# Context of batches 1 to 7 loaded in 32-by-32 blocks and turned on VectorE

## The chip, the core and the metric

The kernel runs on one core of a Trainium2 chip. Its engines are TensorE (PE in the profile, with PEld for its weight loads), VectorE (DVE), ScalarE (ACT), GpSimd (POOL) and SyncE (SP), which here issues every DMA. The metric is the device time of one launch in microseconds, lower is better. Each engine runs its own instructions in order, and they wait for each other by semaphores.

## What is computed

One layer of cross-attention with a residual, then a gated sign-weight feed-forward with a residual. The stage that this change touches is the projection of the keys and values, whose input is the context and the normalised latents:

```python
hidden_states = jnp.concatenate([context, latents], axis=1)      # (8, 256, 512)
q = (latents @ Wq).reshape(b, q_len, N_KV_HEADS, N_GROUPS, HEAD_DIM)
k = (hidden_states @ Wk).reshape(b, kv_len, N_KV_HEADS, HEAD_DIM)
v = (hidden_states @ Wv).reshape(b, kv_len, N_KV_HEADS, HEAD_DIM)
scores = jnp.einsum('bqhgd,bkhd->bhgqk', q, k) * scale
attn = jax.nn.softmax(scores.astype(jnp.float32), axis=-1).astype(q.dtype)
out = jnp.einsum('bhgqk,bkhd->bqhgd', attn, v)
...
x = x + _L0_xattn_ref(_layernorm(x, axis=-1), ctx_4096, Wq, Wk, Wv, Wo)
x = x + _L0_ffn_ref(_layernorm(x, axis=-1), weight, bias, gate_w, in_scale, out_scale)
```

There are 8 batches of 128 context rows and 128 latent rows, 512 wide; 32 query heads and 4 key heads of 128.

## The kernel before

Everything is in fp32. A product is made from a high part (rounded to fp32r) and a low part (the rest) of both operands, with three of the four partial products: 12 matmuls of 128x512 for one product of the value projection.

The program has stages: the value projection ("V stage", up to about 61 us), the key projection ("K stage", to about 106 us), and then, for each key head and each half of its query heads, attention and output projection, with the feed-forward woven into the last round. The order of each engine is written out by hand; nothing is scheduled by a program.

In the V stage a batch `b` has two products, number `n = 2b` for the context (`cT`) and `n = 2b + 1` for the latents (`xT`). Both need their input with the features on the partitions, while memory has the rows there, so each is turned first:

- SP loads the raw context `craw[:, b]` (`load_c`, L244) and the raw latents `acc[:, b]` (`load_x`, L241), 256 KB each in 128 runs of 2 KB. The order on SP's queue is: `craw` 0, the first two quarters of Wv, `acc` 0, the other two quarters, then `craw` and `acc` of batches 1 to 7 in turn, with Wk (1 MB) after batch 4, then the gate weights and the bias, and only then the stores of V.
- PE turns the context with four transpositions against the identity into `t_bank[1]` (`ct_transpose`, L1105), and the normalised latents `y` into `t_bank[0]` (`xt_transpose`, L1097). Behind the context's product of batch `b` stands the context's transposition of `b + 1`, behind the latents' product the latents' transposition of `b + 1`.
- ACT copies the turned tile to the high part (`ct_half`, `xt_half`), DVE writes the rest (`ct_rest`, `xt_rest`). All such copies and subtractions go through two helpers and have the lines L563 (ACT) and L821 (DVE).
- PE makes the product (`product`, L1088) in one of two banks. ACT copies its high part into `v_stage`, DVE the rest, which raises `proj_lo`. Product `n` waits until the bank is free: `proj_lo` of product `n - 2`.
- After both products of a batch SP stores `v_stage[:, b % 2]` to `v_park` (L277). ACT may write a batch into `v_stage` only when the store of batch `b - 2` has landed: it waits for `v_parked` ahead of its first instruction of batch `b`, which is `ct_half(b + 1)`.
- DVE's order in batch `b` is: `ct_rest(b+1)`, layer statistics of `b + 2`, the rest of product `2b`; `xt_rest(b+1)`, layer norm of `b + 2`, the rest of product `2b + 1`. POOL makes 1/sqrt from the variance in six small instructions.

Of the kernel before, what the change touches and what calls it, by code (L numbers as in the profile page):

```python
# [22 lines left out]
HI, LO = 0, 1  # L23
# [4 lines left out]
def xattn_ffn(nc, x, ctx, wq, wk, wv, wo, ffn_w, ffn_b, gate_w, in_cs, out_cs, out):  # L28
# [6 lines left out]
    P = 128  # L35
    B, T, D = x.shape
    HC = D // P
# [16 lines left out]
    QB = P // 32  # L54

    es = ExitStack()
    with es:
        def sb(stack, name, shape, dt=fp32):
            return stack.enter_context(nc.sbuf_tensor(name, shape, dt))

        def sem(name):
            return es.enter_context(nc.semaphore(name))
# [39 lines left out]
        with ExitStack() as pre:  # L102
            cT = sb(pre, "cT", [P, 2, HC, B * T], f32r)
            wv_pair = sb(pre, "wv_pair", [P, 2, HC, D], f32r)
            craw = sb(pre, "craw", [P, B, D])
            wk_pair = sb(pre, "wk_pair", [P, 2, HC, D], f32r)
            v_stage = sb(pre, "v_stage", [P, 2, G, 2, KC, P], f32r)
            k_stage = sb(pre, "k_stage", [P, 2, HALF, 2, QB, KC, 32], f32r)

        with ExitStack() as att:  # L110
# [17 lines left out]
        with ExitStack() as fin:  # L128
# [9 lines left out]
        s_bank, t_bank, proj_bank = bank[0:2], bank[2:4], bank[6:8]  # L138
# [9 lines left out]
        c_in = [sem(f"c_in{b}") for b in range(B)]  # L148
# [17 lines left out]
            sem(n) for n in ("stats_ready", "mv_ready", "rstd_ready", "rstd_step", "shift_ready",  # L166
                             "y_ready"))

        xt_ready, xt_hi, xt_lo, ct_ready, ct_hi, ct_lo = (
            sem(n) for n in ("xt_ready", "xt_hi", "xt_lo", "ct_ready", "ct_hi", "ct_lo"))  # L170

        proj_ready, proj_hi, proj_lo = sem("proj_ready"), sem("proj_hi"), sem("proj_lo")

# [58 lines left out]
        def _(sp):  # L232
# [8 lines left out]
                sp.dma_start(acc[:, b, :], x[b]).then_inc(x_in[b], 16)  # L241

            def load_c(b):
                sp.dma_start(craw[:, b, :], ctx[b]).then_inc(c_in[b], 16)  # L244

            def load_wq(g, quad, c):
                cols = bass.ds(g * (QUADS * QH * P) + quad * QH * P, QH * P)
# [10 lines left out]
            def load_v(g, b):  # L258
                sp.dma_start(words(vg[:, b, :, :, :]), v_park[g, :, b, :, :, :]).then_inc(v_in[b], 16)

            load_c(0)
            for c in range(HC):
                if c == 2:
                    load_x(0)
                sp.dma_start(raw_a[:, c, :], wv[c * P:(c + 1) * P, :]).then_inc(wv_in[c], 16)
            for b in range(1, B):
                load_c(b)
                load_x(b)
                if b == 4:
                    sp.dma_start(raw_b[:, :, :], wk.rearrange("(c p) n -> p c n", p=P)  # L270
                                 ).then_inc(wk_in, 16)
# [287 lines left out]
        def _(act):  # L559
            open_loop(act, *exp_ready, p_hi, o_hi)  # L560

            def copy(dst, src):
                return nc.scalar.activation(dst, src, ACT.Copy)  # L563
# [9 lines left out]

            def ct_half(b):

                act.wait_ge(ct_ready, b + 1)
                copy(cT[:, HI, :, b * T:(b + 1) * T],
                     t_bank[1][:, :].rearrange("p (c t) -> p c t", c=HC)).then_inc(ct_hi, 1)

            for c in range(HC):  # L580
                act.wait_ge(wv_in[c], 16)
# [4 lines left out]
            for b in range(B):  # L586
                if b >= 2:
                    act.wait_ge(v_parked[b % 2], 16 * (b // 2))
                for kc in range(KC):
                    n = 2 * b + kc  # L590
# [17 lines left out]
            for u in range(G * NHALF):  # L608
                if 3 <= u < 6:
# [4 lines left out]
                    rows = slice(32 * (u - 3), 32 * (u - 3) + E)  # L614
# [3 lines left out]
                for kc in range(KC):  # L618
                    n = 2 * B + 2 * u + kc
# [197 lines left out]
        def _(dve):  # L817
            open_loop(dve, *max_ready, rsum_ready, *turned, o_lo, acc_ready)

            def subtract(dst, a, b):  # L820
                return nc.vector.tensor_tensor(dst, a, b, ALU.subtract)  # L821

            def layer_stats(i, b):
                nc.vector.bn_stats(stats[:, i % 2], acc[:, b, :]).then_inc(stats_ready, 1)  # L824
                dve.wait_ge(stats_ready, i + 1)
                nc.vector.bn_aggr(mv[:, i], stats[:, i % 2]).then_inc(mv_ready, 1)

            def layer_norm(i, b):

                dve.wait_ge(rstd_ready, 2 * i + 2)  # L830
                nc.vector.tensor_scalar(y[:, i % 2], acc[:, b, :], mv[:, i, 0:1], rstd[:, i:i + 1],
                                        ALU.subtract, ALU.mult).then_inc(y_ready, 1)

            def xt_rest(b):
                dve.wait_ge(xt_hi, b + 1)
                part = xT[:, :, :, b * T:(b + 1) * T]
                subtract(part[:, LO], t_bank[0][:, :].rearrange("p (c t) -> p c t", c=HC),
                         part[:, HI]).then_inc(xt_lo, 1)

            def ct_rest(b):  # L840
                dve.wait_ge(ct_hi, b + 1)
                part = cT[:, :, :, b * T:(b + 1) * T]
                subtract(part[:, LO], t_bank[1][:, :].rearrange("p (c t) -> p c t", c=HC),
                         part[:, HI]).then_inc(ct_lo, 1)

            ct_rest(0)
            dve.wait_ge(x_in[0], 16)
            layer_stats(0, 0)
            for c in range(HC):
                if c == 2:  # L850
# [4 lines left out]
                subtract(wv_pair[:, LO, c, :], raw_a[:, c, :], wv_pair[:, HI, c, :]  # L855
                         ).then_inc(wv_lo, 1)
            xt_rest(0)
            layer_norm(1, 1)
            for b in range(B):
                for kc in range(KC):  # L860
                    n = 2 * b + kc
                    if b + 1 < B:
                        (ct_rest, xt_rest)[kc](b + 1)
                    if b + 2 < B:
                        if kc == 0:
                            dve.wait_ge(x_in[b + 2], 16)
                            layer_stats(b + 2, b + 2)
                        else:
                            dve.wait_ge(xt_ready, b + 1)
                            layer_norm(b + 2, b + 2)  # L870
                    dve.wait_ge(proj_hi, n + 1)
                    subtract(v_stage[:, b % 2, :, LO, kc, :],
                             proj_bank[n % 2][:, :].rearrange("p (g d) -> p g d", g=G),
                             v_stage[:, b % 2, :, HI, kc, :]).then_inc(proj_lo, 1)
            for u in range(G * NHALF):
# [4 lines left out]
                for kc in range(KC):  # L880
                    n = 2 * B + 2 * u + kc
# [191 lines left out]
        def _(pe):  # L1073
# [19 lines left out]
            def xt_transpose(b):  # L1093
                pe.wait_ge(y_ready, b + 1)
                pe.wait_ge(xt_lo, b)
                for c in range(HC):
                    last = nc.tensor.transpose(t_bank[0][:, c * T:(c + 1) * T],  # L1097
                                               y[:, b % 2, c * P:(c + 1) * P], ident[:, :])
                last.then_inc(xt_ready, 1)
# [11 lines left out]
            for b in range(B):  # L1111

                for kc, (src, lo_sem) in enumerate(((cT, ct_lo), (xT, xt_lo))):
                    n = 2 * b + kc
                    if n == 0:
                        pe.wait_ge(ct_hi, 1)
                    else:
                        pe.wait_ge(lo_sem, b + 1)
                    if n >= 2:
                        pe.wait_ge(proj_lo, n - 1)  # L1120
                    product(proj_bank[n % 2][:, :],
                            lambda s, c: src[:, s, c, b * T:(b + 1) * T],
                            lambda s, c: wv_pair[:, s, c, :], HC,
                            (wv_hi, wv_lo) if n == 0 else None,
                            {1: lambda: pe.wait_ge(ct_lo, 1), 2: lambda: xt_transpose(0)}
                            if n == 0 else {}
                            ).then_inc(proj_ready, 1)
                    if b + 1 < B:
                        (ct_transpose, xt_transpose)[kc](b + 1)

            pe.wait_ge(gate_in, 16)
            pe.wait_ge(xt_lo, B)
# [6 lines left out]
            for u in range(G * NHALF):  # L1139

                g, half = divmod(u, NHALF)
                for kc, src in enumerate((cT, xT)):
                    n = 2 * B + 2 * u + kc
# [227 lines left out]
```

## Time and profile before

| | us |
|---|---|
| median of 3 runs | 694.87 (694.29 to 695.62) |
| the profiled execution, its own time | 695.12 |
| its span, first to last instruction | 693.3 |
| PE busy in the span | 672.2 (97%) |
| DVE / ACT / POOL busy | 444.4 / 354.7 / 304.5 |

The times below are counted from the span's start. In the rows, a line of the timeline is start, duration, engine, line, operation, what is written from what; in brackets the idle time before it and what ended it. SPq is the queue of SP: the duration there is that of the issue, not of the transfer.

### The profile page before, as it was taken

The page shows a single profiled execution, that of the slowest core. Times are in us where ns is not written, and L with a number is a line of the kernel's source. Part 1 is how long each engine was busy: PE and PEld are TensorE (multiplying, and loading weights), DVE is VectorE, ACT ScalarE, POOL GpSimd, SP SyncE. Part 2 cuts the span into 40 slices and gives each one's busy share as a digit, 9 for nine tenths or more (in the row PEclk, how much of TensorE's full clock was granted, in tenths as well). Part 3 has the DMA queues.
Part 4 walks back from the last instruction along what each step waited for, and adds up shares of the span by engine and source line. Part 5 has one row for each costly group of instructions (what it writes and reads, how often), then busy time and mean ns, then how long its engine had stood idle before and what let it go on. Part 6 is the DMA issues. An engine that isn't in the chain of part 4 may idle for free.

```text
span 693.3 us, 10261 instructions
## 1 busy us (share of the span) xinstructions
PE 672.2 (97%) x3368; PEld 563.6 (81%) x3368; DVE 444.4 (64%) x726; ACT 354.7 (51%) x889; POOL 304.5 (44%) x272
## 2 busy tenths in 40 slices
PE   6999999999999999999999999999999999989995
PEld 4888887878888888888888888888888888768774
DVE  4553233666776766777767777667766676667763
ACT  3344322755565456555655564465556545646542
POOL 4135000542374246324633463345236438854773
PEclk9999999999999999999999999999999999999998
DMA  9556447689668876656698866667877665454411
GB/s 322 216 206 242 197 197 251 200 259 265 202 183 269 264 252 202 222 187 182 198 289 256 243 207 198 194 185 249 260 253 238 190 191 206 166 141 139 146 46 45
DMA packets 90692, 144.84 MB, mean 209 GB/s; under 512 B 15192, under 2 KB 47960, under 8 KB 89616
## 3 DMA queue, kind: packets, MB, share of 16 engines
q1 hardware_dynamic: 90640, 144.19, 64.9%
q8 instruction: 27, 0.44, 0.3%
q14 instruction: 25, 0.20, 0.1%
HBM read 91.60 MB, written 52.56 MB: 208 GB/s over the span
## 4 chain that ended last, share of the span: by engine, by line
PE 86%; DMA 4%; DVE 3%; POOL 2%; ACT 2%; issue 1%; SPq 1%; ACTq 0%; DVEq 0%
PE bank L1088 47%; PE bank L1202 23%; PE bank L1187 11%; DMA p_park<-p_turned 2%; PE bank L1278 2%; POOL p_low L459 1%; DMA kg<-k_park 1%; DVE bank L929 1%; DMA acc<-in_x 1%; POOL wo_pair L473 1%; ACT prob L646 1%; PE bank L1097 1%; DVE stats L824 1%; PE bank L1252 1%; PE bank L1237 1%
## 5 line engine op out<-in xcount | busy, mean ns | idle before, releaser
L459 POOL TENSOR_TENSOR p_low<-p_low,p_high 128x1024 fp32r<-128x1024 f32 x64 | 153.8, 2403 | 252.3 <-ACT p_high L563 252.2
L1202 PE MATMUL bank<-wo_pair,oT 128*128 128x512 f32 x768 | 188.5, 393 | 4.3 <-DVE oT L821 3.3
L1088 PE MATMUL bank<-xT,wq_pair 128*128 128x512 f32 x768 | 185.7, 391 | 0.0
L1202 PEld LDWEIGHTS bank<-wo_pair,oT 128*128 128x128 f32 x768 | 139.3, 188 | 34.2 <-issue 5.7
L1088 PEld LDWEIGHTS bank<-xT,wq_pair 128*128 128x128 f32 x768 | 140.2, 188 | 26.8
L563 ACT ACTIVATE oT<-bank 128x512 fp32r<-128x512 f32 x64 | 38.3, 598 | 197.4 <-DVE bank L929 197.4
L646 ACT ACTIVATE prob<-bank,nmax 128x256 f32<-128x256 f32 x256 | 119.1, 471 | 32.7 <-DVE nmax L899 32.5
L914 DVE STREAM_TRANSPOSE p_turned<-prob 128x512 f32<-128x512 f32 x128 | 91.0, 711 | 61.1 <-ACT prob L646 61.1
L1088 PEld LDWEIGHTS bank<-kg,qT 128*128 128x128 f32 x768 | 108.0, 190 | 11.5 <-DMA kg<-k_park 1.2
L1088 PE MATMUL bank<-kg,qT 128*128 128x256 f32 x768 | 111.6, 283 | 1.5 <-DMA kg<-k_park 0.8
L899 DVE TENSOR_REDUCE nmax<-bank 128x2 f32<-128x512 f32 x128 | 87.6, 686 | 38.3 <-PE bank L1088 38.3
L929 DVE TENSOR_TENSOR bank<-bank,r_all 128x512 f32<-128x512 f32 x64 | 69.0, 1078 | 39.2 <-PE bank L1187 39.2
L1187 PE MATMUL bank<-p_high,vg 128*128 128x512 f32 x256 | 69.0, 391 | 0.0
L563 ACT ACTIVATE p_high<-p_low 128x1024 fp32r<-128x1024 f32 x64 | 67.7, 1057 | 0.2
L467 POOL TENSOR_TENSOR wq_pair<-raw_a,wq_pair 128x512 fp32r<-128x512 f32 x28 | 36.4, 1300 | 58.7 <-ACT wq_pair L563 58.7
L1187 PEld LDWEIGHTS bank<-p_high,vg 128*128 128x128 f32 x256 | 47.6, 188 | 9.6
L921 DVE TENSOR_TENSOR acc<-bank,acc 128x512 f32<-128x512 f32 x64 | 44.2, 690 | 12.8 <-PE bank L1202 12.8
L646 ACT ACTIVATION_READ_ACCUMULATOR prob<-bank,nmax 128x1 f32 x256 | 50.4, 197 | 0.0
L892 DVE SCALAR_TENSOR_TENSOR qT<-bank,qT 128x512 fp32r<-128x512 f32 x64 | 43.6, 682 | 10.3 <-ACT qT L634 10.1
L821 DVE TENSOR_TENSOR oT<-bank,oT 128x512 fp32r<-128x512 f32 x64 | 44.1, 689 | 4.1
L634 ACT ACTIVATE qT<-bank 128x512 fp32r<-128x512 f32 x64 | 37.9, 593 | 10.7 <-PE bank L1088 10.7
L473 POOL TENSOR_TENSOR wo_pair<-raw_b,wo_pair 128x512 fp32r<-128x512 f32 x32 | 40.5, 1302 | 0.2 <-ACT wo_pair L563 0.2
(89 smaller groups left out, 601.0 us busy)
## 6 DMA issues: line engine op xcount, KB each, us to landing
p_park<-p_turned SPq DMA_DIRECT2D x64, 512.0 KB, 3.7
p_low<-p_park SPq DMA_DIRECT2D x64, 512.0 KB, 4.9
r_all<-r_park SPq DMA_DIRECT2D x64, 256.0 KB, 4.5
v_park<-v_stage SPq DMA_DIRECT2D x8, 1024.0 KB, 4.1
raw_a<-in_L_xattn_Wq SPq DMA_DIRECT2D x32, 256.0 KB, 5.2
raw_b<-in_L_xattn_Wo SPq DMA_DIRECT2D x32, 256.0 KB, 4.9
k_park<-k_stage SPq DMA_DIRECT2D x8, 1024.0 KB, 3.8
kg<-k_park SPq DMA_DIRECT2D x32, 256.0 KB, 5.4
```

Of the source, the lines that this page charges most:

```text
L459: nc.gpsimd.tensor_tensor(part, part.bitcast(fp32), p_high[:, :].rearrange("p i c q -> p (i c q)"), ALU.subtract).then_inc(p_lo, 1)
L473: nc.gpsimd.tensor_tensor(wo_pair[:, LO, h, :], raw_b[:, h, :], wo_pair[:, HI, h, :], ALU.subtract).then_inc(wo_lo, 1)
L563: return nc.scalar.activation(dst, src, ACT.Copy)
L646: ins = nc.scalar.activation(prob[:, p, j], s_bank[p][:, j * KEYS:(j + 1) * KEYS], ACT.Exp, bias=nmax[:, p, j:j + 1], accum_out=esum[:, t ...
L821: return nc.vector.tensor_tensor(dst, a, b, ALU.subtract)
L899: nc.vector.tensor_reduce(nmax[:, p], s_bank[p][:, :].rearrange("p (h k) -> p h k", h=2), AX.X, ALU.max, negate=True).then_inc(max_ready[p ...
L914: nc.vector.transpose(p_turned[:, t % 2, :, 2 * p:2 * p + 2, :].rearrange("p k h q -> p h k q"), prob[:, p].rearrange("p h (k e) -> p h k ...
L921: nc.vector.tensor_tensor(acc[:, t], wo_bank[:, :], acc[:, t], ALU.add).then_inc(acc_ready, 1)
L929: nc.vector.tensor_tensor(o, o, r_all[:, t % 2].rearrange("p (i q) h -> p i h q", i=QB), ALU.mult).then_inc(o_scaled, 1)
L1088: last = nc.tensor.matmul(dst, left(a, c), right(b, c), start=(n == 0), stop=(n == 3 * chunks - 1))
L1187: last = nc.tensor.matmul(av_bank[:, :], vg[:, t, vs, kc, :], ps[:, :, kc, :], start=(n == 0), stop=(n == 3 * KC - 1))
L1202: last = nc.tensor.matmul(wo_bank[:, :], oT[:, s, h, :], wo_pair[:, w, h, :], start=((s, w) == TERMS[0] and h == 0), stop=((s, w) == TERMS ...
```

## The change

The context of batch 0 is loaded and turned as before. For batches 1 to 7:

- the load takes 32-by-32 blocks to where a turn inside each block completes the whole transposition. It is four DMAs per batch, one for each group of 32 partitions, each of 32 x 16 runs of 32 floats (128 bytes). The bytes are the same.
- PE's `ct_transpose(b)` is gone; DVE has a new instruction `ct_turn(b)`, one transposition of 128x512 in 32x32 blocks from `craw` to a new tile `cturn` (two batches deep, 2 KB a partition each).
- ACT's `ct_half` and DVE's `ct_rest` read `cturn` in place of the PSUM bank. `ct_turn(1)` stands ahead of the second layer norm, `ct_turn(b + 2)` right behind `ct_rest(b + 1)`.

`cturn` shares its memory with `k_stage`, which is first written in the K stage.

```diff
             def load_c(b):
-                sp.dma_start(craw[:, b, :], ctx[b]).then_inc(c_in[b], 16)
+                if b == 0:
+                    sp.dma_start(craw[:, b, :], ctx[b]).then_inc(c_in[b], 16)
+                    return
+
+
+                blocks = ctx[b].rearrange("(k s) (c i r) -> i s c k r", s=32, i=QB, r=32)
+                for i in range(QB):
+                    rows = craw[32 * i:32 * (i + 1), b, :].rearrange("s (c k r) -> s c k r", c=HC, k=QB)
+                    sp.dma_start(rows, blocks[i]).then_inc(c_in[b], 16)
...
             def ct_half(b):
 
-                act.wait_ge(ct_ready, b + 1)
-                copy(cT[:, HI, :, b * T:(b + 1) * T],
-                     t_bank[1][:, :].rearrange("p (c t) -> p c t", c=HC)).then_inc(ct_hi, 1)
+                if b == 0:
+                    act.wait_ge(ct_ready, 1)
+                    src = t_bank[1][:, :]
+                else:
+                    act.wait_ge(ct_turned, b)
+                    src = cturn[:, b % 2]
+                copy(cT[:, HI, :, b * T:(b + 1) * T], src.rearrange("p (c t) -> p c t", c=HC)
+                     ).then_inc(ct_hi, 1)
...
+            def ct_turn(b):
+                dve.wait_ge(c_in[b], 16 * QB)
+                nc.vector.transpose(cturn[:, b % 2].rearrange("p (m s) -> p m s", s=32),
+                                    craw[:, b].rearrange("p (m r) -> p m r", r=32)
+                                    ).then_inc(ct_turned, 1)
+
...
             xt_rest(0)
+            ct_turn(1)
             layer_norm(1, 1)
             for b in range(B):
                 for kc in range(KC):
                     n = 2 * b + kc
                     if b + 1 < B:
                         (ct_rest, xt_rest)[kc](b + 1)
+                        if kc == 0 and b + 2 < B:
+                            ct_turn(b + 2)
...
-                    if b + 1 < B:
-                        (ct_transpose, xt_transpose)[kc](b + 1)
+                    if kc == 1 and b + 1 < B:
+                        xt_transpose(b + 1)
```

On SP's queue, at the start of the program, before (`craw` is the raw context, `acc` the raw latents):

```order
L244 DMA craw<-in_ctx 128x512
L265 DMA raw_a<-in_L_xattn_Wv 128x512 x2
L241 DMA acc<-in_x 128x512
L265 DMA raw_a<-in_L_xattn_Wv 128x512 x2
L244 DMA craw<-in_ctx 128x512
L241 DMA acc<-in_x 128x512
```

and now:

```order
L248 DMA craw<-in_ctx 128x512
L276 DMA raw_a<-in_L_xattn_Wv 128x512 x2
L244 DMA acc<-in_x 128x512
L276 DMA raw_a<-in_L_xattn_Wv 128x512 x2
L255 DMA craw<-in_ctx 32x16x32 x4
L244 DMA acc<-in_x 128x512
```

Each context load from batch 1 on is four issues in place of one, and everything on the queue behind it stands 3 issues further back for each batch.

On PE, around the first context product of a batch (rows with `y` are the latents' transposition), before:

```order
L1088 MATMUL bank<-wv_pair,xT 128x512 x11
L1097 MATMUL bank<-ident,y 128x128 [waits xt_lo,y_ready]
L1097 MATMUL bank<-ident,y 128x128 x3
L1088 MATMUL bank<-wv_pair,cT 128x512 [waits proj_lo,ct_lo]
L1088 MATMUL bank<-wv_pair,cT 128x512 x11
L1105 MATMUL bank<-ident,craw 128x128 [waits ct_lo,c_in2]
L1105 MATMUL bank<-ident,craw 128x128 x3
```

and now:

```order
L1114 MATMUL bank<-wv_pair,xT 128x512 x11
L1123 MATMUL bank<-ident,y 128x128 [waits xt_lo,y_ready]
L1123 MATMUL bank<-ident,y 128x128 x3
L1114 MATMUL bank<-wv_pair,cT 128x512 [waits proj_lo,ct_lo]
L1114 MATMUL bank<-wv_pair,cT 128x512 x11
L1114 MATMUL bank<-wv_pair,xT 128x512 [waits proj_lo,xt_lo]
```

The two rows of L1105 are gone, and the latents' product follows the context's product directly.

On DVE, from the end of the first batch's preparation (`xT` of batch 0) to the rest of the first product (`v_stage`), before:

```order
L821 TENSOR_TENSOR xT<-bank,xT 128x4x128 [waits xt_hi]
L831 TENSOR_SCALAR y<-acc,mv,rstd 128x512 [waits rstd_ready]
L821 TENSOR_TENSOR cT<-bank,cT 128x4x128 [waits ct_hi]
L824 BN_STATS stats<-acc 128x6 [waits x_in2]
L826 BN_AGGR mv<-stats 128x2 [waits stats_ready]
L821 TENSOR_TENSOR v_stage<-bank,v_stage 128x4x128 [waits proj_hi]
```

and now:

```order
L837 TENSOR_TENSOR xT<-bank,xT 128x4x128 [waits xt_hi]
L858 STREAM_TRANSPOSE cturn<-craw 128x512 [waits c_in1]
L847 TENSOR_SCALAR y<-acc,mv,rstd 128x512 [waits rstd_ready]
L837 TENSOR_TENSOR cT<-cturn,cT 128x4x128 [waits ct_hi]
L858 STREAM_TRANSPOSE cturn<-craw 128x512 [waits c_in2]
L840 BN_STATS stats<-acc 128x6 [waits x_in2]
L842 BN_AGGR mv<-stats 128x2 [waits stats_ready]
L837 TENSOR_TENSOR v_stage<-bank,v_stage 128x4x128 [waits proj_hi]
```

Two turns stand ahead of the first `v_stage` row, and one more ahead of each later one of a context product.

## Rows read from the trace of the kernel before

**Rows 1.** The page, part 4: the chain that ended last, share by engine.
```profile
PE 86%; DMA 4%; DVE 3%; POOL 2%; ACT 2%; issue 1%; SPq 1%; ACTq 0%; DVEq 0%
```

**Rows 2.** The chain in order of time, start of program: start, duration, what.
```profile
4.00 5.72 DMA acc<-in_x
...
9.75 0.70 DVE stats L824
...
11.15 0.78 PE bank L1097 x4
...
13.34 3.05 PE bank L1088 x12
16.40 0.44 PE bank L1097 x4
16.83 2.78 PE bank L1088 x12
19.61 0.44 PE bank L1105 x4
```

**Rows 3.** The timeline of 12 to 16 us, DVE and ACT.
```profile
12.60 0.69 DVE L821 TENSOR_TENSOR xT<-bank,xT 128x512 fp32r<-128x512 f32 x1 [0.30 <-ACT xT L563]
...
13.24 0.55 DVE L831 TENSOR_SCALAR y<-acc,mv,rstd 128x512 f32<-128x512 f32 x1
...
13.84 0.59 ACT L563 ACTIVATE v_stage<-bank 128x512 fp32r<-128x512 f32 x1
13.98 0.69 DVE L821 TENSOR_TENSOR cT<-bank,cT 128x512 fp32r<-128x512 f32 x1 [0.19 <-ACT cT L563]
14.58 0.69 DVE L824 BATCH_NORM_STATS2 stats<-acc 128x6 f32<-128x512 f32 x1
...
15.40 0.66 DVE L821 TENSOR_TENSOR v_stage<-bank,v_stage 128x512 fp32r<-128x512 f32 x1
```

**Rows 4.** The page, part 5: DVE's block transposition of the attention stage.
```profile
L914 DVE STREAM_TRANSPOSE p_turned<-prob 128x512 f32<-128x512 f32 x128 | 91.0, 711 | 61.1 <-ACT prob L646 61.1
```

**Rows 5.** The timeline, SP's queue: issues of one context load, bias, V stores.
```profile
3.53 0.43 SPq L244 DMA_DIRECT2D craw<-in_ctx  x1
...
12.22 0.35 SPq L273 DMA_DIRECT2D bias_b<-in_L_ffn_bias  x1
...
19.27 19.70 SPq L277 DMA_DIRECT2D v_park<-v_stage  x4
```

**Rows 6.** DMA issues of 3.5:3.9, 12.2:12.6, 19.1:20 us; last number: us to landing.
```profile
craw<-in_ctx SPq DMA_DIRECT2D x1, 256.0 KB, 5.5
...
bias_b<-in_L_ffn_bias SPq DMA_DIRECT2D x1, 256.0 KB, 8.6
...
v_park<-v_stage SPq DMA_DIRECT2D x1, 1024.0 KB, 4.1
```

**Rows 7.** DMA queue of 124.5:124.9, 127.0:127.6, 14:19 us: packets, MB, share of 16 engines.
```profile
DMA packets 86, 0.00 MB, mean 3 GB/s; under 512 B 86, under 2 KB 86, under 8 KB 86
...
q1 hardware_dynamic: 86, 0.00, 12.1%
...
DMA packets 199, 0.20 MB, mean 340 GB/s; under 512 B 0, under 2 KB 199, under 8 KB 199
...
q1 hardware_dynamic: 199, 0.20, 98.4%
...
q1 hardware_dynamic: 1092, 2.03, 105.0%
```

**Rows 8.** Stretches at the end: PE, PEld, DVE, ACT, POOL busy, PEclk, DMA share, GB/s.
```profile
680.00:682.00 2.00, 0.21 (x1) 0.18 (x1) 1.57 (x4) 0.82 (x3) 1.44 (x2) 0.61 0.29 109
682.00:684.00 2.00, 1.63 (x6) 1.35 (x6) 0.55 (x2) 0.28 (x1) 0.00 (x0) 0.50 0.00 0
684.00:686.00 2.00, 2.00 (x6) 1.53 (x5) 1.05 (x2) 1.09 (x2) 0.00 (x0) 0.50 0.00 0
686.00:688.00 2.00, 2.00 (x7) 1.59 (x7) 0.53 (x2) 0.00 (x0) 0.00 (x0) 0.68 0.00 0
```

More of the change, by code:

```diff
@@ L107, in xattn_ffn @@
             v_stage = sb(pre, "v_stage", [P, 2, G, 2, KC, P], f32r)
+            with ExitStack() as turned_ctx:
+                cturn = sb(turned_ctx, "cturn", [P, 2, D])
             k_stage = sb(pre, "k_stage", [P, 2, HALF, 2, QB, KC, 32], f32r)
@@ L167, in xattn_ffn @@
                              "y_ready"))
-        xt_ready, xt_hi, xt_lo, ct_ready, ct_hi, ct_lo = (
-            sem(n) for n in ("xt_ready", "xt_hi", "xt_lo", "ct_ready", "ct_hi", "ct_lo"))
+        xt_ready, xt_hi, xt_lo, ct_ready, ct_turned, ct_hi, ct_lo = (
+            sem(n) for n in ("xt_ready", "xt_hi", "xt_lo", "ct_ready", "ct_turned", "ct_hi", "ct_lo"))
         proj_ready, proj_hi, proj_lo = sem("proj_ready"), sem("proj_hi"), sem("proj_lo")
@@ L842, in ct_rest @@
                 part = cT[:, :, :, b * T:(b + 1) * T]
-                subtract(part[:, LO], t_bank[1][:, :].rearrange("p (c t) -> p c t", c=HC),
-                         part[:, HI]).then_inc(ct_lo, 1)
+                src = t_bank[1][:, :] if b == 0 else cturn[:, b % 2]
+                subtract(part[:, LO], src.rearrange("p (c t) -> p c t", c=HC), part[:, HI]
+                         ).then_inc(ct_lo, 1)
             ct_rest(0)
```

## The prediction

> **What bounds the kernel now.** I read the chain that ended last first: 86% of the span is PE's [rows 1], and in order of time the V stage is one line of PE pieces without a gap from 13.34 us on: product, four transpositions, product, four transpositions [rows 2]. A removed piece of that line is time won, if nothing else comes late. A transposition of four costs the line 0.44 us, a product 2.78 us; a product that starts after a wait costs 3.05 us, 0.27 more, since the array fills again (I use 0.25). Before 13.34 us the chain is not PE's: it runs through the landing of the latents of batch 1 at 9.72 us (4.00 + 5.72), DVE's statistics behind it, the first layer norm, the transposition of `xT` at 11.15. So the start is bound by the DMA queue.
>
> **What a load costs on the queue.** The context of batch 1 lands at 3.53 + 5.5 = 9.03 us and the bias at 12.22 + 8.6 = 20.82 [rows 5, 6]. Between them lie 13 loads of 256 KB, Wk (four times as much) and the bias: 18 units in 11.79 us, 0.655 us each, and the engines are never free in between (105.0% for 14 to 19 us) [rows 7]. The change leaves the bytes and makes 2048 packets of 128 bytes, 128 for each of 16 DMA engines, out of 128 packets of 2 KB, 8 for each. The trace of before has no packet of that size. Its neighbours: 86 packets of at most 16 bytes took 12.1% of 0.4 us x 16 = 0.77 us, 9.0 ns each; 199 packets of 1 KB took 98.4% of 0.6 x 16 = 9.45 us, 47.5 ns each [rows 7]. An eighth of a 1 KB packet shouldn't take longer than the whole, so 9.0 and 47.5 ns are the bounds. The straight line between them gives 9.0 + 112 x 38.5 / 1008 = 13.3 ns. I take that, as 128 bytes are much nearer to the 16-byte row. A context load then costs 128 x 13.3 ns, plus four times 9 ns for the semaphore packets of its four DMAs, 1.74 us: 1.09 us more than now, seven times.
>
> The trace's own rows thus make the small runs about 2.7 times as slow as the long ones. The Trainium skill says in "DMA: Bandwidth & Descriptors", section "Specifications", that a transfer reaches line rate from 512 bytes on, and that below this the engine does a read-modify-write. No row shows or denies that. It speaks against this change, and what it would do here is the second rival below.
>
> **The change part by part.**
>
> 1. *Transpositions gone from PE.* Seven times four. The first (batch 1) gives nothing: after it PE waited for `xT` of batch 0, which DVE had at 13.29 (12.60 + 0.69), and started at 13.34 [rows 2, 3]. It turns into waiting. The other six stand between products without a gap: 6 x 0.44 = 2.64 us won.
>
> 2. *First latents later.* The load of batch 1's context stands ahead of the latents of batch 1, on which the chain waits at 9.72. They land 1.09 us later, and the whole of PE's line with them: 1.09 us lost. Issue isn't the limit there: three more issues of 0.43 us plus 0.04 end at 4.9 us, while their data starts to move at about 8.4.
>
> 3. *DVE's turns.* Seven at 0.71 us, the price of the same operation on the same size in attention [rows 4]. In a batch of 6.0 us DVE has some 4 us of work, so the sum fits; what matters is the order. In batch 0 two of them stand ahead of the rest of product 0. Walk through it, 1.09 later than now: `xT` rest done 14.38, turn 1 to 15.1, ACT's `ct_half(1)` from 15.1 instead of ahead of 13.84, so its copy of product 0 ends at 16.2. DVE: `ct_rest(1)` 15.7, turn 2 16.3, statistics 16.95, rest of product 0 from 17.8 to 18.5 (now 15.40 to 16.06 [rows 3]). Product 2 waits for it: PE is ready at 14.43 + 3.05 + 0.44 = 17.92 and starts at 18.51. Lost: 0.59 + 0.25 to fill again = 0.84 us. From batch 1 on the turn is one batch ahead of its use, and the same walk leaves 0.4 us or more of slack.
>
> 4. *The V stores behind the loads.* This is the largest term. The store of batch 0 now is issued at 19.27 and lands 4.1 us later at 23.37, right behind the bias (20.82 plus 1 MB) [rows 5, 6]. The queue is first in, first out, so with seven loads of 1.09 more it lands at 23.37 + 7.63 = 31.0. ACT may not begin batch 2 before it: behind that wait stand `ct_half(3)` and the copy of product 4; on DVE behind those `ct_rest(3)`, turn 4, statistics 4, rest of product 4. Now that store lands before ACT gets there and the wait costs nothing. After: ACT's two copies 31.0 to 32.0, with DVE's `ct_rest(3)` from 31.65, turn 4 32.25, statistics 32.9 and 33.6, rest of product 4 from 33.75 to 34.43: 3.45 us after the landing. Product 6 needs that bank. PE is ready at 18.51 + 3.05 + 2.79 + 0.44 + 2 x 2.79 + 0.44 = 30.81 and starts at 34.47. Lost: 3.66 + 0.25 = 3.91 us. Later stores land in time: the next one is right behind (33.6, used by ACT about then), the queue is empty after that. SP's 21 more issues at 0.47 end at 12.6 + 9.9 = 22.5, past the 19.27 at which V's store is ready, but the data ahead of it moves until 28.4, which hides that.
>
> 5. *The clock.* It is granted in full through the V stage. At the end it fell, in a stretch with PE busy for 0.21 us of 2, and stood at half (1.2 in place of 2.4 GHz) for 2 x (0.78 + 1 + 1 + 0.64) = 6.8 us of four stretches [rows 8]. A wait of 3.7 us is as empty. There PE kept waiting after the fall; here it goes on at once, so I take half of that, 3.4 us at half clock, in which products that take 1.6 to 2 times as long lose about 1.5 us.
>
> ACT's and DVE's reads from `cturn` instead of PSUM are of equal size and hidden. After the V stage nothing changes, and PE's line carries the difference to the end (the K stage has no DMA or DVE wait).
>
> Sum: -2.64 + 1.09 + 0.84 + 3.91 + 1.5 = +4.7 us. On the profiled execution's own 695.12 us this gives 699.8; that execution is 0.25 us above the median of the runs, less than the doubt in any term.
>
> **Rivals.**
>
> *Cheap packets: the change doesn't lose, and ends below the time before.* If a 128-byte packet costs the lower bound of 9.0 ns, a load costs 1.19 us, 0.53 more. The latents come 0.53 late, term 3 stays 0.84, the store lands at 27.1, and product 6 could start at 30.6 where PE is ready at 30.25: 0.35 + 0.25. No clock loss. -2.64 + 0.53 + 0.84 + 0.60 = -0.7, 694.4 us. It decides at about 9.6 ns a packet, where the sum is zero; each nanosecond on top costs 0.128 x 8 = 1.0 us. For it: small packets in the trace do go at 9.0 ns; against: those carry 16 bytes, and the size has a price in every other row.
>
> *Dear packets.* If small reads cost double (26.6 ns), a load costs 3.44 us, 2.8 more; the store lands at 42.9, product 6 starts at 46.4 where PE is ready at 32.5. -2.64 + 2.8 + 0.84 + 14.1 + 1.5 = +16.6, 711.7 us. At the upper bound of 47.5 ns it is +36, 731 us. For it: the 16-byte packets are writes, and reads from memory may not overlap as well in small pieces. Against: the 2 KB reads lie on the line of the other two rows to within 3 ns (1092 packets of 14 to 19 us took 84 us; of them 991 of 2 KB, 83.9 ns each, where the line gives 86.6) [rows 7]. The Trainium skill's read-modify-write below 512 bytes ("DMA: Bandwidth & Descriptors", "Specifications"), taken as twice the price, would end here too.
>
> *No clock loss.* All as forecast, but the wait leaves the clock alone: +3.2, 698.3 us.
>
> **How the numbers follow.** Forecast with or without the clock loss, 11 to 17 ns a packet: 0.55 (+1.5 to +8.5 us). Cheap packets, below 11 ns: 0.17, of which most within 0.2% (1.4 us, about what a measurement of this kernel can tell from no change) and hardly any below, since even the cheapest case wins only 0.7: 0.14 same, 0.03 faster. Dear packets, above 17 ns: 0.28, half of it below 26. Slower 0.83. The range takes in the lower bound's 694.4 and reaches into the dear case to 712.
>
> **What would show it.** Context loads landing 1.1 us further apart from each other; the first `xT` transposition on PE at 12.2 instead of 11.15; a wait of PE of 0.6 us ahead of product 2 (about 18 us) and one of 3 to 4 us at about 31 us, with ACT waiting for the V store just before and PEclk below 1 behind it; batches of 6.0 us after that. Wrong would be the forecast if the wait at 31 us is missing (packets under 10 ns) or over 8 us long (twice the price), or if waits stand in every batch, which would be DVE or the context loads and not the store.

## The result: 707.62 us, 1.8% slower, and the profile after

| | before | changed |
|---|---|---|
| median of 4 runs, us | 694.58 (694.29 to 695.62) | 707.62 (706.4 to 709.1) |
| ratio to before | | 1.0183, interval 1.0168 to 1.0198 |
| span of the profiled execution | 693.3 | 706.1 |
| mean granted clock of TensorE | 0.995 | 0.988 |

The forecast was 699.8 us, 4.7 above the profiled execution before; the change costs 13.0 us by the medians and 12.8 by the spans. The sign was right, the size was not, and the time lies inside the range.

The chain in order of time of the changed kernel, to be read beside [rows 2] (start, duration, what; up to 30.57 the chain is SP's issues, most rows of it left out):

```profile
3.53 0.72 SPq L255
...
6.32 1.04 SPq L244
...
7.40 0.58 SPq L255
...
28.41 0.64 SPq L255
...
29.09 0.63 SPq L244
...
30.57 5.93 DMA v_park<-v_stage
36.52 0.64 ACT cT L574
37.19 0.69 DVE cT L837
37.88 0.62 DVE cturn L858
38.50 0.59 DVE stats L840
...
39.29 0.59 DVE v_stage L837
...
40.02 8.13 PE bank L1114 x24
48.15 0.44 PE bank L1123 x4
48.58 5.58 PE bank L1114 x24
```

Before, the chain was PE's from 13.34 us on. Now it runs through SP's issues of the loads up to 30.6 us, then through the first V store (L288), which lands at 36.50, then through ACT and DVE in just the order that the prediction walked through, and only at 40.02 is it PE's again. From 48 us on a batch is 5.58 + 0.44 = 6.02 us, where two products and two transpositions took 6.43 before (2.80 + 0.44 + 2.75 + 0.44).

PE's waits of the changed kernel between 12 and 80 us (engine, line, for whom: us in total, times, longest):

```profile
PE bank L1114 <- DVE v_stage L837: 10.8, 2, 10.2
PE bank L1114 <- DVE xT L837: 0.4, 1, 0.4
```

and the granted clock after it (the columns are those of [rows 8]):

```profile
36.00:38.00 2.00, 0.00 (x0) 0.00 (x0) 0.81 (x2) 1.48 (x3) 0.00 (x0) 0.50 0.96 372
38.00:40.00 2.00, 0.00 (x0) 0.02 (x1) 1.97 (x5) 1.24 (x3) 0.54 (x2) 0.50 0.06 24
40.00:42.00 2.00, 1.99 (x5) 1.63 (x6) 1.02 (x3) 0.00 (x0) 1.01 (x5) 0.50 0.00 0
42.00:44.00 2.00, 2.00 (x7) 1.54 (x6) 2.00 (x4) 0.00 (x0) 0.00 (x0) 0.50 0.27 97
44.00:46.00 2.00, 2.00 (x8) 1.65 (x7) 0.57 (x2) 0.60 (x1) 1.07 (x4) 0.73 1.02 392
```

The two waits are 0.60 us ahead of product 2 and 10.2 us ahead of product 6. The clock stood at half (1.2 GHz) when product 6 began, and that product took 5.34 us:

```profile
40.02 5.34 PE L1114 MATMUL bank<-wv_pair,cT 128*128 128x512 f32 x12 [10.20 <-DVE v_stage L837]
```

The V stage ends at 72.25 us instead of 61.00. Of the 11.25 us the terms make 11.1: 0.12 at the start (the first latents' product at 13.46 instead of 13.34), 0.60 + 0.24 ahead of product 2, 10.20 ahead of product 6, 0.25 to fill again, 2.30 for product 6 at the lower clock, less 6 x 0.44 = 2.64. The other 1.6 us come later, see the end of the section on the forecast.

The packets cost what was forecast where block loads move alone, and more on the average. A stretch of the changed kernel's queue with block loads alone, 25.0 to 25.5 us, and below it the whole of 8 to 30 us:

```profile
DMA packets 502, 0.06 MB, mean 125 GB/s; under 512 B 502, under 2 KB 502, under 8 KB 502
...
q1 hardware_dynamic: 502, 0.06, 80.0%
...
DMA packets 13738, 4.16 MB, mean 189 GB/s; under 512 B 12458, under 2 KB 12458, under 8 KB 13738
...
q1 hardware_dynamic: 13738, 4.16, 88.1%
```

80.0% of 0.5 us x 16 is 6.4 us, 12.7 ns a packet (13.3 were taken). And the engines are only busy for 80% of it: there the queue is not what limits. From 8 to 30 us the packets took 88.1% of 22 us x 16 = 310 us. With 84 ns for each of the 1280 long ones (the time of [rows 7]) 16 ns are left for a short one, an estimate; the surplus sits in a few stretches (18 to 19 us: 203 short and 86 long ones in 100.1% of 1 us x 16). SP's issues, which the chain runs through:

```profile
14.06 2.62 SPq L255 DMA_DIRECT2D craw<-in_ctx  x4
16.73 0.62 SPq L244 DMA_DIRECT2D acc<-in_x  x1
17.39 0.43 SPq L281 DMA_DIRECT2D raw_b<-in_L_xattn_Wk  x1
...
30.57 12.40 SPq L288 DMA_DIRECT2D v_park<-v_stage  x3
```

Four block loads keep SP for 2.62 us (0.58 for the first, 0.64 for each other, 0.04 between them), and the plain load behind them takes 0.62 too, where the same instruction took 0.43 before. Five of the seven batches of loads take SP 3.33 us. The first takes 3.87, and the one right behind Wk 5.22, with DMA engines busy all the time from 18 to 24 us: there SP was held by the queue. SP came to the first V store at 30.57, not at 22.5.

### The profile page after: what moved, and what is told of

It is laid out like the page before. It is cut to its first block, busy times and chain, and to the rows that moved or that the text cites. A ratio compares the mean times of both kernels' runs of the same rounds, so it can differ in the third digit from the quotient of the medians.

```text
span 706.1 us, 10226 instructions
## 1 busy us (share of the span) xinstructions
PE 673.0 (95%) x3340; PEld 562.3 (80%) x3340; DVE 448.8 (64%) x733; ACT 354.6 (50%) x889; POOL 304.8 (43%) x272
## 4 chain that ended last, share of the span: by engine, by line
PE 82%; SPq 4%; DMA 4%; DVE 3%; POOL 2%; ACT 2%; issue 1%; ACTq 0%; DVEq 0%
PE bank L1114 45%; PE bank L1228 23%; PE bank L1213 11%; SPq L255 3%; DMA p_park<-p_turned 2%; PE bank L1304 2%; DMA kg<-k_park 1%; POOL p_low L470 1%; SPq L244 1%; DVE bank L955 1%; DMA v_park<-v_stage 1%; POOL wo_pair L484 1%; ACT prob L662 1%; PE bank L1278 1%; PE bank L1263 1%
## 5 line engine op out<-in xcount | busy, mean ns | idle before, releaser
L947 DVE TENSOR_TENSOR acc<-bank,acc 128x512 f32<-128x512 f32 x64 | 44.2, 690 | 12.9 <-PE bank L1228 12.8
L1114 PE MATMUL bank<-wv_pair,cT 128*128 128x512 f32 x96 | 29.5, 457 | 12.5 <-DVE v_stage L837 10.8
```

The costliest lines, as they stand in the source:

```text
L947: nc.vector.tensor_tensor(acc[:, t], wo_bank[:, :], acc[:, t], ALU.add).then_inc(acc_ready, 1)
L1114: last = nc.tensor.matmul(dst, left(a, c), right(b, c), start=(n == 0), stop=(n == 3 * chunks - 1))
```

## The experiments

Theory A: the loss is the late first V store, which stood behind the loads on SP's queue, and what follows from it (the wait of PE and the lower clock); DVE's turns cost 0.85 us once. Rivals: the turns cost PE in every batch; the small packets slow the whole stage; and, for the size, whether SP's time is priced by the DMA, by its runs or by its form. The kernels ran on several chips, each chip with its own runs of the kernel before, so each time is compared with the kernel before on its own chip.

### Plain loads with DVE's turns

```diff
-                blocks = ctx[b].rearrange("(k s) (c i r) -> i s c k r", s=32, i=QB, r=32)
-                for i in range(QB):
...
+                sp.dma_start(craw[:, b, :], ctx[b]).then_inc(c_in[b], 16)
...
-                dve.wait_ge(c_in[b], 16 * QB)
+                dve.wait_ge(c_in[b], 16)
```

> The changed kernel with each context load as before the change, one DMA of 128 rows of 2 KB; DVE turns and all else as changed. The turned context is then not the transposed one (its 32-by-32 blocks stand in the wrong places), so the output is wrong and only the time counts. Theory A (all loss is in the loads): 694.6 - 2.6 + 0.85 = 692.8 us, with the first latents landing at 9.7 us and a wait of 0.6 us ahead of product 2. Rival C (DVE's turns cost on PE's line in every batch): 694.6 us or more, and waits of PE for DVE in several batches.

This kernel leaves out the placing of the blocks, so its context is wrong and only its time counts. Measured: 693.9 us against 696.17 us of the kernel before, ratio 0.9966 (0.9950 to 0.9982), 2.3 us faster. The V stage ends at 59.57 us; PE's only waits for DVE in it are these (rows of later stages left out):

```profile
PE bank L1106 <- DVE v_stage L829: 0.6, 1, 0.6
PE bank L1106 <- DVE xT L829: 0.5, 1, 0.5
```

So DVE's turns do what they were meant to do, and cost 0.6 us once, as forecast. The whole loss is in the loads.

### The block loads alone

```diff
-                sp.dma_start(craw[:, b, :], ctx[b]).then_inc(c_in[b], 16)
+                (the block loads of the change)
...
-                pe.wait_ge(c_in[b], 16)
+                pe.wait_ge(c_in[b], 16 if b == 0 else 16 * QB)
```

> The kernel before with the block loads alone: four DMAs of 512 runs of 128 bytes for each of batches 1 to 7, and PE still transposes (what it transposes is the context with its blocks elsewhere, so the output is wrong). Theory A: the first V store is issued at about 30.6 us and lands at about 36.5, PE stands from about 29.5 to 39.3 us, the clock falls, 694.6 + 9.6 + 2.5 = 706 to 708 us: the loads alone cost more than the whole change does. Rival C (turns on DVE are a part of the loss): under 703 us.

Measured in one run: 711.98 us, 15.8 over the median of before on that chip (here too the context is wrong). SP's queue and PE's wait:

```profile
33.28 11.66 SPq L285 DMA_DIRECT2D v_park<-v_stage  x3
...
PE bank L1096 <- DVE v_stage L829: 10.6, 1, 10.6
```

SP came to the store even later, at 33.28: three of its groups of loads took 3.00, 3.78 and 3.53 us instead of 2.62, and two plain loads 1.74 and 2.21. The loads alone cost more than the whole change, so DVE's turns are no part of the loss. The expected 706 to 708 was 4 us too low. It had 9.6 us for the wait and 2.5 for refill and clock; in the trace these are 10.6 and 1.8, the first latents' product starts 1.7 us late (15.02 instead of 13.34), and the rest comes after the V stage, as in the changed kernel. Why SP was held longer than in the changed kernel was not tried.

### Other cuts of the same load: what SP's time depends on

Three kernels are the kernel before with another `load_c` for batches 1 to 7; PE transposes as before.

```diff
 four long: 4 DMAs, 32 partitions x 1 run of 2 KB
+                for i in range(QB):
+                    part = slice(32 * i, 32 * (i + 1))
+                    sp.dma_start(craw[part, b, :], ctx[b, part, :]).then_inc(c_in[b], 16)
 two short: 2 DMAs, 128 partitions x 8 runs of 128 bytes
+                to = craw[:, b, :].rearrange("p (m i r) -> p m i r", i=2, r=32)
+                rows = ctx[b].rearrange("p (m i r) -> p m i r", i=2, r=32)
+                for i in range(2):
+                    sp.dma_start(to[:, :, i], rows[:, :, i]).then_inc(c_in[b], 16)
 four mid: 4 DMAs, 64 partitions x 4 runs of 256 bytes, in the same manner with r=64
```

> The kernel before with each context load of batches 1 to 7 as four DMAs of 32 partitions, rows of 2 KB, 32 runs each: four times the DMAs and no small packet; nothing else changes. If the issue is priced at 0.44 us plus 0.5 ns a run, an issue takes 0.46 us, SP is done with the loads at about 22 us and the data keeps up with it: the first V store lands at about 27 us, PE does not wait, 694 to 696 us. If four DMAs on a quarter of the partitions cost 0.64 us whatever their runs, SP is done at 28 to 30 us, the wait comes back, 703 us or more.

> The kernel before with each context load of batches 1 to 7 as two DMAs of 128 partitions x 8 runs of 128 bytes: 1024 runs each, the same 2048 small packets a batch as the change, with half the DMAs; every block lands where it did before. If SP's issue is priced by runs, an issue takes about twice the 0.65 us of 512 runs, 1.3 us, and SP is done with the loads at about the same 30 us: 706 to 708 us as with four. If it is priced by the DMA (0.43 to 0.65 us whatever its runs), SP is done at about 20 us, the store lands at about 30 us and the time is 697 to 699 us.

> The kernel before with each context load of batches 1 to 7 as four DMAs of 64 partitions x 4 runs of 256 bytes, 256 runs each; every block lands where it did before. If an issue costs 0.44 us plus 0.5 ns a run, it takes 0.57 us; SP is done with the loads at 26 to 27 us, the first V store lands at about 31 us and PE waits some 3 us: 698 to 701 us. If the issue is priced by the form (a pattern with three dimensions on the memory side, 0.63 us in both forms seen), it takes 0.63 us, SP is done at about 29 us, 702 us or more.

SP's timeline of one batch each (context, then latents), of four long, two short and four mid in this order:

```profile
10.53 1.82 SPq L249 DMA_DIRECT2D craw<-in_ctx  x4
12.39 0.42 SPq L241 DMA_DIRECT2D acc<-in_x  x1
```

```profile
10.29 1.50 SPq L250 DMA_DIRECT2D craw<-in_ctx  x2
11.83 1.11 SPq L241 DMA_DIRECT2D acc<-in_x  x1
12.98 1.26 SPq L250 DMA_DIRECT2D craw<-in_ctx  x2
14.28 1.23 SPq L241 DMA_DIRECT2D acc<-in_x  x1
```

```profile
10.00 2.50 SPq L251 DMA_DIRECT2D craw<-in_ctx  x4
12.55 0.60 SPq L241 DMA_DIRECT2D acc<-in_x  x1
```

| load of one batch | runs per DMA | us per issue | first V store issued at | time of one run | above before, same chip |
|---|---|---|---|---|---|
| 4 x (32 x 2 KB) | 32 | 0.42 | 21.25 | 698.24 | 2.7 |
| 2 x (128 x 8 x 128 B) | 1024 | 0.61 | 27.50 | 704.05 | 7.9 |
| 4 x (64 x 4 x 256 B) | 256 | 0.60 | 27.98 | 705.46 | 10.0 |
| 4 x (32 x 16 x 128 B), PE transposing | 512 | 0.63 | 33.28 | 711.98 | 15.8 |
| 4 x (32 x 16 x 128 B), the change | 512 | 0.63 | 30.57 | 707.93 | 13.4 |

(us per issue is the time of a group that was not held, less 0.04 between issues.) The number of runs is not the price: 1024 cost no more than 256. The three cuts with several short runs a partition cost 0.60 to 0.63, the ones with a single run 0.42. But several runs a partition aren't enough: the load of Wk has four runs of 2 KB on each of 128 partitions, 512 runs as in a block load, and took 0.43 us among the block loads (the row at 17.39 above). So what these runs separate is short runs (128 and 256 bytes) from runs of 2 KB; lengths between, and other differences of the patterns, were not tried.

The rule that I put into the expectations, 0.44 us plus 0.5 ns a run, is wrong, and four-mid's 705.46 missed its 698 to 701. The expectation of two-short had only two cases, priced by runs (706 to 708) or by the DMA (697 to 699), and its 704.05 is neither. In two-short the issue itself was the second, but SP did not get ahead for it: the latents' load behind each pair held SP, for 0.9 to 1.4 us in five batches and for 3.1 and 4.0 us in the first and the one behind Wk. The DMA engines were busy for 0.89 to 1.05 of every stretch of 3 or 4 us from 8 us on. There the data is the limit. Its store landed at 33.7 us, 2.7 later than the 31.0 that the forecast had for a queue that never stands idle: by the reckoning above a short packet took 15.6 ns on the average in this kernel, and 2.3 ns more on 128 packets of each engine in seven batches are 2.1 us of that, an estimate. SP stays only 3.8 to 4.0 us ahead of the landing outside of the two held batches, where it was 8.6 us ahead before [rows 6].

Four-long shows that neither the count of DMAs nor their quarter of the partitions is at fault: no late store, and PE's V stage without a wait for it. It missed its 694 to 696 all the same. Of the 2.7 us 1.7 stand ahead of 16 us: the first latents land 0.4 us later, and then four matmuls of PE took 1.71 us instead of 0.94 and four transpositions 0.85 instead of 0.44, for which no run here shows the cause.

### The stores between the loads

The changed kernel with the order of SP's queue altered and nothing else.

```diff
             for b in range(1, B):
                 load_c(b)
                 load_x(b)
+                if b in (4, 5):
+                    store_v(b - 4)
-                if b == 4:
-                    (load of Wk)
+                if b == 6:
+                    (load of Wk)
+                    store_v(2)
```

> The changed kernel with another order on SP's queue only: the store of batch 0's V stands behind the loads of batch 4, that of batch 1 behind batch 5, Wk and the store of batch 2 behind batch 6. The same 28 block loads, the same issues, the same packets. Theory A (the loss is the late first V store, and with it the clock): PE's 10.2 us wait ahead of product 6 goes to under 1 us and the clock stays full, so 10.2 + 2.3 us come back; what is left is -2.6 us for six transpositions, +0.6 + 0.25 for the wait ahead of product 2, +0.1 at the start: 692 to 694 us. Rival B (small packets or DVE's turns slow the stage as a whole): waits stay in other places, 700 us or more.

Measured: 700.24 against 696.17, ratio 1.0065 (1.0048 to 1.0081): two thirds of the loss are gone with the same loads and packets. The expected 692 to 694 did not come, and the reason is seen in the chain and in PE's waits:

```profile
33.26 9.80 DMA v_park<-v_stage
...
46.57 7.36 PE bank L1120 x24
```

```profile
PE bank L1120 <- DVE v_stage L843: 4.3, 2, 3.7
```

The wait ahead of product 6 is gone, but the store of batch 2 stood behind Wk (1 MB) and a batch of block loads and took 9.8 us to land; PE waited 3.7 us and the clock fell again (two products in 7.36 instead of 5.6). My order had made the same fault in another place. That is the mechanism of theory A once more, and not the rival's.

### Wk behind the context loads, and later turns

```diff
             for b in range(1, B):
                 load_c(b)
                 load_x(b)
+                if b >= 4:
+                    store_v(b - 4)
+            (load of Wk)
```

> The changed kernel with only SP's order altered, as the run with the stores between the loads, but with Wk (1 MB) behind all context loads, and the stores of batches 0 to 3 behind the loads of batches 4 to 7. Theory A (what is left of the loss there is the one store that stood behind Wk: 3.7 us of waiting, 0.25 to fill again and 1.8 us of half clock): the wait at about 42 us is gone, PE waits only 0.6 us for DVE ahead of product 2, and the time is 1.5 to 2 us below the kernel before. Rival: a store behind four block DMAs lands late by itself, so a wait of 1 us or more is left in every batch, and the time is at or above the kernel before.

The second kernel adds: batch 1 loaded and transposed as before, and

```diff
-                        if kc == 0 and b + 2 < B:
-                            ct_turn(b + 2)
...
                              v_stage[:, b % 2, :, HI, kc, :]).then_inc(proj_lo, 1)
+                    if kc == 0 and b + 2 < B:
+                        ct_turn(b + 2)
```

> The run with Wk last, with two more edits: batch 1's context is loaded and transposed on PE as in the kernel before (that transposition stood in a wait for xT), and each turn on DVE stands behind the rest of the context's product instead of ahead of it. Expected: the 0.6 us wait ahead of product 2 and the 0.25 us to fill again are gone, the start is that of the kernel before, so it wins another 0.8 to 1.0 us and ends 2.6 us below the kernel before. Rival: the later turn delays ct_half and moves the wait elsewhere; then no gain over the run with Wk last.

Measured: 697.41 and 696.84 against 695.51, ratios 1.0027 (1.0014 to 1.0039) and 1.0015 (0.9999 to 1.0031). Neither gained, where 1.5 to 2 and 2.6 us had been expected. Their V stages ran at 6.02 us a batch up to 47 us, and then a store was late again, now behind Wk, bias and the first quad of Wq (chain of the first and of the second):

```profile
45.57 8.83 DMA v_park<-v_stage
```

```profile
43.93 9.09 DMA v_park<-v_stage
...
55.54 7.34 PE bank L1118 x24
```

The 0.6 us ahead of product 2 is gone in the second kernel, as expected. Both waited the same 2.0 us for that store. In the second the granted clock then fell to half and two products took 7.34 us, in the first it stayed full and two products took 5.77. By the second's chain, without the 2.0 us of waiting and the slow products behind it the stage would end some 2 us ahead of the kernel before.

### Spaced loads: a version that beats both

Two last pairs, each with its control: the order alone, on the kernel before. The two kernels with block loads keep the two changes of the second kernel above, so batch 1 is loaded plainly and six batches in blocks. First Wk behind the store of batch 3, gate weights behind 4, bias behind 5, Wq behind 6:

> The run with late turns, with the rest of SP's order mended too: no load of more than one piece stands ahead of a V store that is soon due. Wk behind the store of batch 3, the gate weights behind that of 4, the bias behind 5, the first quad of Wq behind 6. Theory A (the one wait left was the store of batch 4 or 5 behind Wk, bias and Wq: 2.0 us, 0.25 to fill again, 1.75 us of half clock): PE has no wait of over 0.3 us from 14 us to the end of the V stage, which ends at about 59 us instead of 61.0, and the time is 2 to 2.6 us below the kernel before. Rival: with each wait removed another store is late; then it stays within 1 us of the kernel before.

> A control: the kernel before, with its plain loads and PE's transpositions, and only SP's order of the run with Wq last. If the gain of that run comes from the order and not from the transpositions, this one gains as much, 2 us or more. By theory A it gains nothing: no V store was late before, so 0 within 0.5 us.

Measured: 696.19 against 696.25 (0.9999, 0.9984 to 1.0014), control 697.34 (1.0017, 1.0008 to 1.0027). The expected 2 to 2.6 us did not come. The V stage had no wait, but Wq was now too late for ACT, which splits it ahead of the K stage's copies:

```profile
58.13 6.24 DMA raw_a<-in_L_xattn_Wq
64.39 2.19 ACT wq_pair L579 x4
```

PE waited 2.3 us for the K stage's bank. In the control, which lost 1.1 us where 0 was expected, it waited 0.9 us there; its V stage too began late, with slow pieces of PE ahead of 14.3 us as in four-long. The last step was to put Wq one store earlier:

```diff
             store_v(5)
-            (load of the bias)
-            store_v(6)
             (loads of Wq)
+            store_v(6)
+            (load of the bias)
             store_v(7)
```

> The run with Wq last, with the first quad of Wq one place earlier on SP's queue: behind the V store of batch 5 instead of 6, and the bias behind that of 6. In that run the V stage had no wait and ended at about 59 us, 2.2 us ahead of the kernel before, but ACT splits Wq ahead of the K stage's copies, and Wq landed at 64.4 us, so that PE waited 2.3 us for the K stage's bank and the clock fell. Theory A: with Wq landing at about 56 us that wait is gone, the K stage starts at about 59 us, and 2.0 to 2.5 us are left of the gain: 0.9965 to 0.997 of the kernel before. Rival: the store of batch 6 lands late behind Wq; then PE waits 1 us or more near 58 us and the gain is under 1 us.

> The control: the kernel before, with its plain loads and PE's transpositions, and SP's order of the spaced run. Its V stage has no late store in either order, so theory A expects 0 within 0.7 us (the control in the order with Wq last lost 1.2 us to the late Wq, which should be gone). If it gains 2 us too, the gain of the spaced run is the order's and not the transpositions'.

Measured: 693.32 us against 695.79, ratio 0.9965 (0.9949 to 0.9982), 2.5 us faster; control 695.22, ratio 0.9989 (0.9976 to 1.0002). The control's interval takes in no change. Against the control, which has the same order, the medians are 1.9 us apart and the V stages 2.06 (58.62 and 60.68), so most of the gain is the transpositions'. The chain of the spaced kernel is PE's again:

```profile
13.42 3.05 PE bank L1118 x12
16.47 0.44 PE bank L1127 x4
16.90 5.58 PE bank L1118 x24
...
53.05 5.58 PE bank L1118 x24
58.62 0.98 PE bank L1166 x8
59.61 55.38 PE bank L1118 x240
```

From 12 to 110 us PE waits for nobody, and the V stage ends at 58.62 us, 2.38 ahead of the 61.00 before: six transpositions of 0.44 us are 2.64, less 0.1 at the start and 0.03 in each pair of products.

## Why the forecast was right or wrong

**What bounds the kernel.** Right. PE's line carries a delay of the V stage to the end, and a transposition is worth 0.44 us when nothing else comes late. The spaced kernel shows it: 2.4 us in the V stage for six.

**Price of a packet.** Right where block loads move alone, 12.7 ns, with 13.3 taken from the line between the 16-byte and the 1 KB rows; somewhat low on the average, which comes out at about 16 ns from 8 to 30 us. The rule of the Trainium skill that I set beside it ("DMA: Bandwidth & Descriptors", "Specifications": no line rate below 512 bytes) holds as to bytes per second, since a 128-byte packet costs 12.7 ns and not a sixteenth of the 2 KB packet's 84; neither this nor the average of about 16 ns is the doubled price, 26.6.

**Step 1, transpositions.** Right, the first one's worth of nothing too.

**Step 2, first latents.** Too large for this run: 1.09 taken, 0.12 measured on PE's line. SP issued that load only at 6.32, and it landed 3.6 us later, right behind the blocks: on the queue 0.25 us later than before. It varies: statistics on it started at 9.99 us in the changed kernel, at 10.58 and 10.82 in the two with the same first loads.

**Step 3, DVE's turns.** Right: 0.60 + 0.24 us, and no wait for a turn from batch 1 on.

**Step 4, the V store.** Here is the error. The wait is the one described, and the way from the landing to PE's start was 3.52 us where 3.47 had been worked out. But what made the store late was SP's issues, which the forecast had put at nothing. The store landed at 36.50, not at 31.0. The sentence that failed is "SP's 21 more issues at 0.47 end at 12.6 + 9.9 = 22.5 ... but the data ahead of it moves until 28.4, which hides that". I took the issue's price from a load with one run a partition [rows 5]. The block load costs 0.63, the plain load behind it 0.62 as well, and SP was held in two batches (2.06 us for one latents' load). Seven batches at 3.33 us, with Wk, gate weights and bias, would end at 28.1, and the two held ones add 2.4: 30.57. The store then also has to wait behind the last loads: 5.9 us to land instead of 4.1. Its wait is 10.2 us and not 3.66. The issue's price is thus 5.6 of the 8.1 us that SP came late; the rest is the queue holding SP, for which Wk ahead of it and the dearer stretches of packets are likely causes, not shown by a run. I had bounded the packet from both sides, and the issue not at all, although it had no row of such a load either.

**Step 5, the clock.** Right in kind, too small: 2.3 us instead of 1.5, so the rival without a clock loss fell. PE was idle for 10 us and began at half clock; the loss is product 6, 5.34 us instead of 3.05. At the 3.7 us of the run with the stores between, close to the wait that was forecast, two products lost 1.8 us, near to the 1.5. But the length of the wait alone does not decide: after 2.0 us the clock fell in one kernel and held in another.

**The sum.** With the measured wait and clock in steps 4 and 5 it gives -2.64 + 1.09 + 0.84 + 10.45 + 2.3 = 12.0, against 11.25 in the V stage and 12.8 in all. So the two terms explain the miss; step 2, 0.97 too large, took some of it back by luck. The 1.6 us after the V stage are not explained by the change: they stand in the first steps of attention, where the chain waits for landings from the parking buffers in each version (7.98 us for one `p_park` store and its load back, 7.12 before; 7.77 for one load of `kg`, 6.85 before, for which PE waits 1.5 us, 0.8 before). That wait was 0.3 us with plain loads and turns, 1.5 with four long loads, 1.9 with Wq last, and 1.9 in the last control, which has only plain loads, so it varies among kernels that have the block loads and those that don't. Why it does was not tried.

**The rivals.** Cheap packets (under 11 ns) and dear ones (above 17) both fell with the measured 12.7 and the average of about 16 ns. What I called dear packets would have come nearer to the size, 711.7 us, for a wrong reason. And the sign named for it, a wait over 8 us long, came true at 10.2 without it: the wait's length can't tell a slow packet from a slow issue.

## What to carry to other kernels

A load that is cut into many short runs has two prices: packets on the DMA engines, and time of the engine that issues it. The second is paid by everything behind it on the queue, so look for the store that frees a buffer, and compare when it is reached with when it is due. If it is late, put it between the loads and spread the large ones, one behind each store: here block loads went from 13 us lost to 2.5 us won by the order and two small moves (batch 1's load left plain, the turns one place later). When a price is taken from a row, check that the row has the form of the new instruction, for the issue as well as for the data.

## What the runs showed of the hardware

- An issue on SP costs 0.42 to 0.43 us for a load with one run of 2 KB a partition, and 0.43 for Wk's with four of them (512 runs in all). It costs 0.60 to 0.63 us with several runs of 128 or 256 bytes a partition, whether 256, 512 or 1024 runs in all. The plain load behind such ones costs 0.60 to 0.63 too, where it is not held. Lengths between 256 bytes and 2 KB were not tried.
- SP runs less far ahead of the data with short runs: a plain load was issued up to 8.9 us ahead of its landing before, and 3.0 to 4.4 us ahead in the changed kernel; with two DMAs of short runs a batch and full DMA engines it was 3.8 to 4.0, and 5.5 and 6.5 in the two batches that were held.
- A 128-byte packet took 12.7 ns of a DMA engine where such packets moved alone; from 8 to 30 us of the changed kernel the average is about 16 ns, if 84 are taken for each 2 KB packet.
- After PE's 10 us of waiting a product of 12 matmuls took 5.34 us, most of it at half clock; after the 3.7 us of the run with the stores between, two products took 7.36 us instead of 5.6. After 2.0 us two products took 7.34 us in one kernel and 5.77, at full clock, in another.
